# A transformer's band mask moved from TensorE to VectorE, and ten maxima steps ahead instead of eight

## What is computed

```python
k = jnp.repeat(k, 2 * NQ // NKV, axis=1)
scores = jnp.einsum('bhqd,bhkd->bhqk', q, k) / math.sqrt(HD)
scores = jnp.where(causal, scores, -jnp.inf)
aw = jax.nn.softmax(scores, axis=-1)
```

```python
mask = (it < jb) | (it > jb + w) | (jb == -1)          # w = 32
sim = jnp.einsum('bhwie,bhwje->bhwij', bq, bk2) * QK_SCALE
sim = jnp.where(mask, -jnp.finfo(sim.dtype).max, sim)
attn = jax.nn.softmax(sim, -1)
out = jnp.einsum('bhwij,bhwje->bhwie', attn, bv2)
```

## Time and profile before

| | us |
|---|---|
| three executions | 3745.32, 3753.55, 3750.16 |
| median | 3750.16 |
| profiled execution | 3755.21 |
| its span, first to last instruction | 3753.5 |
| second attention in it, about | 1107 to 1622 |
| transformer in it, about | 1695 to 3735 |

### The profile page before, as it was taken

One profiled execution on the slowest core, in us unless ns is written; L12 is line 12 of the kernel. 1 busy time (PEld: TensorE's weight loads), 2 busy tenths in 40 slices (PEclk: granted clock), 3 DMA queues, 4 the chain that ended last, 5 costly groups with the idle time before them and its releaser, 6 DMA issues. The chain is left out here.

```text
span 3753.5 us, 73312 instructions
## 1 busy us (share of the span) xinstructions
PE 3066.9 (82%) x23925; PEld 1648.9 (44%) x23925; DVE 2241.2 (60%) x3755; ACT 2086.3 (56%) x3805; POOL 1286.9 (34%) x1223
## 2 busy tenths in 40 slices
PE   2788886249638888836999999999999999999997
PEld 1332332113312232314665565566556556655653
DVE  6888887652347777764555555545555555555553
ACT  1477676012105666624666666666666666666664
POOL 0000000014225556514543453344335334534540
PEclk6588779579858999978999999999999999999998
DMA  5221121124231211123111111111111111111111
GB/s 198 82 84 53 60 72 67 48 52 112 55 43 28 38 35 34 34 64 104 42 45 42 41 52 30 47 39 48 30 48 53 30 42 44 49 31 52 38 35 41
DMA packets 195374, 200.80 MB, mean 53 GB/s; under 512 B 119109, under 2 KB 125909, under 8 KB 190250
## 3 DMA queue, kind: packets, MB, share of 16 engines
q1 hardware_dynamic: 193938, 195.86, 19.1%
q10 hardware_dynamic: 1080, 0.25, 0.0%
HBM read 100.23 MB, written 29.46 MB: 35 GB/s over the span
## 5 line engine op out<-in xcount | busy, mean ns | idle before, releaser
L2427 POOL TENSOR_TENSOR tr_t<-tr_t 128x512 f32<-128x512 f32 x384 | 488.8, 1273 | 707.4 <-DVE tr_t L2271 707.0
L2434 POOL TENSOR_TENSOR tr_nq<-tr_t,tr_rn 128x512 f32<-128x512 f32 x384 | 392.5, 1044 | 393.4 <-ACT tr_rn L2167 393.4
L1638 DVE TENSOR_REDUCE attn_mp<-attn_ps 128x1 f32<-128x512 f32 (+3 forms) x660 | 394.1, 656 | 143.1 <-PE attn_ps L1494 64.1
L2132 ACT ACTIVATE tr_pr<-tr_ps 128x768 f32<-128x768 f32 x264 | 213.9, 810 | 375.6 <-PE tr_ps L1954 375.2
L2270 DVE TENSOR_TENSOR tr_t<-tr_ps,tr_tab 128x512 f32<-128x512 f32 x384 | 263.3, 686 | 245.8 <-ACT tr_sq L2141 245.8
L2280 DVE TENSOR_TENSOR tr_o<-tr_ps,tr_rd 128x384 f32<-128x384 f32 (+1 forms) x264 | 144.0, 545 | 426.8 <-ACT tr_rd L2157 419.0
L1969 PE MATMUL tr_ps<-tr_w,tr_xs 128*128 128x512 f32 x768 | 372.6, 607 | 29.5 <-DVE tr_xs L2298 26.4
L684 DVE TENSOR_REDUCE attn_mcol<-attn_ps 128x1 f32<-128x512 f32 x548 | 357.4, 682 | 49.4 <-PE attn_ps L529 39.4
L1600 ACT ACTIVATE attn_pr<-attn_ps 128x768 f32<-128x768 f32 (+2 forms) x352 | 295.3, 870 | 150.7 <-PE attn_ps L1521 149.8
L668 ACT ACTIVATE attn_pr<-attn_ps 128x512 f32<-128x512 f32 x512 | 272.7, 600 | 88.1 <-DVE attn_ps L706 68.9
L1954 PE MATMUL tr_ps<-tr_qT,tr_kT 64*128 64x96 f32 (+1 forms) x4224 | 301.8, 283 | 0.0
(11 more groups left out here) (260 smaller groups left out, 5082.7 us busy)
## 6 DMA issues: line engine op xcount, KB each, us to landing
tr_v<-tr_va SPq DMA_DIRECT2D x144, 192.0 KB, 2.6
attn_ka<-scratch_kp SPq DMA_DIRECT2D x72, 294.0 KB
tr_v<-tr_va SPq DMA_DIRECT2D x144, 128.0 KB, 2.4
moe_cb<-scratch_combineT SPq DMA_DIRECT2D x32, 512.0 KB
tr_w<-in_w_half SPq DMA_DIRECT2D x12, 1024.0 KB
tr_v<-tr_va SPq DMA_DIRECT2D x48, 256.0 KB, 2.4
scratch_kp<-proj_parts SPq DMA_DIRECT2D x36, 256.0 KB
attn_km<-scratch_kp SPq DMA_DIRECT2D x72, 98.0 KB
```

What stands on the lines that cost most here:

```text
L1638: dve.tensor_reduce(dst, src, AX.X, ALU.max).then_inc(maxed, 1)
L2427: pool.tensor_tensor(t12[:, slot, i, 0, :], t12[:, slot, i, 0, :], t12[:, slot, i, 1, :], ALU.add).then_inc(summed, 1)
L2434: pool.tensor_tensor(nq[:, slot, i, :].rearrange("p (h e) -> p h e", e=DH), t12[:, slot, i, 0, :].rearrange("p (h e) -> p h e", e=DH), rn[ ...
```

## The change

In the transformer the mask matmuls go. `scores` starts its own accumulation and waits for `masked` of the step before instead of `exp_done`. VectorE gets a new `mask(n, j, s)`, first in its step: it adds `band` (now f32, one copy, broadcast over the two banks) to the scores in PSUM and writes 128 x 768 into `pr`. ScalarE's `exps` now waits for `masked`, works in place in `pr`, and stands after `copy_v` instead of at the head of the step. The second load of the band, its cast and `stage_ident` go.

In the second attention `LEAD_STEPS` is 10 instead of 8, and `negate_rows` stands at a = 14, behind the output's copy, instead of at a = 16.

```diff
-LEAD_STEPS = 8
+LEAD_STEPS = 10
...
                         elif a == 14:
                             copy_out(2 * kv + 1, 1, kv)
-                        elif a == 16:
+                        if a == 14:
                             negate_rows(kv + 1, (s + 1) % 2, kv)
...
-        band32 = st.sb("band32", [P, 2, 2, NPAIR * QT])
-        band = st.sb("band", [P, 2, 2, NPAIR * QT], BF16)
+        band = st.sb("band", [P, 2, NPAIR * QT])
...
-            sp.dma_start(band32[:, 0, :, :], d["band"]).then_inc(loaded_const, 16)
-            for half in range(2):
-                sp.dma_start(band32[half * DH:(half + 1) * DH, 1, :, :], d["band"][(1 - half) * DH:(2 - half) * DH]
-                             ).then_inc(loaded_const, 16)
+            sp.dma_start(band[:], d["band"]).then_inc(loaded_const, 16)
...
-                at_least(pe, exp_done, NQT * n + s)
+                at_least(pe, masked, NQT * n + s)
...
-                pe.sem_inc(scores_begun, 1)
-                for e in range(2):
-                    for half in range(2):
-                        row, out = half * DH, (half ^ e) * DH
-                        pe.matmul(ps[out:out + DH, SC0 + e, 0:NPAIR * QT], identb[row:row + DH, row:row + DH],
-                                  band[row:row + DH, e, 1 if s == 0 else 0, :], start=True, stop=True,
-                                  tile_position=(row, out), skip_group_check=True)
...
-                                       qT[rows, p, s * QT:s * QT + width], start=False, stop=True,
-                                       skip_group_check=True)
+                                       qT[rows, p, s * QT:s * QT + width], start=True, stop=True)
...
             def exps(n, j, s):
-                act.wait_ge(scores_done, NQT * n + s + 1)
-                act.activation(pr[:, (j + s) % 2, :, :], ps[:, SC0:SC0 + 2, 0:NPAIR * QT], ACT.Exp,
-                               scale=QK_SCALE).then_inc(exp_done, 1)
+                act.wait_ge(masked, NQT * n + s + 1)
+                act.activation(pr[:, (j + s) % 2, :, :], pr[:, (j + s) % 2, :, :], ACT.Exp, scale=QK_SCALE
+                               ).then_inc(exp_done, 1)
...
                 for s in range(NQT):
-                    exps(n, j, s)
...
                         copy_v(n + 1, PROJ_NEXT_AT[s])
+                    exps(n, j, s)
...
+            def mask(n, j, s):
+                dve.wait_ge(scores_done, NQT * n + s + 1)
+                seen = band[:, 1 if s == 0 else 0, :].unsqueeze(1).broadcast_to((P, 2, NPAIR * QT))
+                dve.tensor_tensor(pr[:, (j + s) % 2, :, :], ps[:, SC0:SC0 + 2, 0:NPAIR * QT], seen, ALU.add
+                                  ).then_inc(masked, 1)
...
                 for s in range(NQT):
+                    mask(n, j, s)
                     if s:
                         outputs(n, s - 1)
...
-            dve.wait_ge(loaded_const, 96)
-            link(dve.tensor_copy(band[:], band32[:]))
+            dve.wait_ge(loaded_const, 64)
```

More of the change, by code:

```diff
@@ L1797, in tile_width, with stage_transformer @@
     return min(QT, S - t * QT)
-def stage_transformer(nc, d, ident, identb, yT):
+def stage_transformer(nc, d, ident, yT):
     with Stage(nc, "tr") as st:
@@ L1845, in stage_transformer @@
         summed, nq_ready, turned, qk_ready = S_("summed"), S_("nq_ready"), S_("turned"), S_("qk_ready")
-        scores_done, exp_done, scores_begun = S_("scores_done"), S_("exp_done"), S_("scores_begun")
+        scores_done, exp_done, masked = S_("scores_done"), S_("exp_done"), S_("masked")
         v_done, v_copied = S_("v_done"), S_("v_copied")
@@ L2483, in build @@
             stage_stash(nc, d, xT, sT)
-        inner, si = scope()
-        with inner:
-            identb = si("identb2", [P, P], BF16)
-            stage_ident(nc, ident, identb)
-            stage_transformer(nc, d, ident, identb, xnT)
-        stage_final(nc, d, ident, xnT)
-def stage_ident(nc, ident, identb):
-    with Stage(nc, "ident") as st:
-        block = st.block()
-        @block.vector
-        def _(dve):
-            dve.tensor_copy(identb[:], ident[:])
+        stage_transformer(nc, d, ident, xnT)
+        stage_final(nc, d, ident, xnT)
 def stage_stash(nc, d, xT, sT):
```

## The result

The change makes the kernel faster: a median of 3706.85 us in four executions (3705.62 to 3709.09) against 3750.66 in four of before, a ratio of 0.9885 with a 95% interval of 0.9868 to 0.9903. The forecast was 3709. A second measurement of the same kernel, later on, gave 3713.69 against 3751.73 (0.9899, 0.9884 to 0.9914). The profiled execution took 3709.1 us, its span is 3707.4.

The account below looks back on a forecast made before the run. TensorE's order was taken to bound the transformer stage, more than half the span. Terms -76.6 + 39.2 - 4 - 3.4 + 4 = -40.8, off the median 3750.16, gave 3709 us; 8-in-10 range 3684 to 3738.

Parts of the forecast that it names:

- gain of the mask: Transformer, TensorE: without the four mask matmuls each of 264 steps saves 0.29 us, -76.6 us.
- new wait: Transformer: TensorE waits for the exponential, now behind the values' copy, in 67 steps at 0.59 us on average, +39.2 us.
- give-back: Transformer, step 3 of 11 feeding passes: the exponential no longer delays ScalarE's key copy, 0.4 us each, -4 us.
- second attention: Second attention: sooner rows gain 0; two more maxima steps and a wait for the negation cost +4 us together.
- start of the stage: Transformer's start: the small cast stage, one band transfer and the band's cast go, -3.4 us.
- VectorE's addition: Transformer: VectorE's mask addition takes 0.96 us a step and TensorE does not wait for it, 0 us.
- 0.1 us on top for weights not loaded ahead: Transformer, steps with TensorE's wait for the exponential: weights load late after it, 0.1 us beyond the 0.51 us wait.
- price of 1.38: VectorE's mask addition: alternative time of 1.38 us, from a multiplication with both inputs in SBUF, instead of 0.96.
- Rival D: Transformer: the in-place exponential from SBUF is much dearer and the 67 waits grow; 3766 at 1.55 us; chance 0.05.
- Rival C: Second attention: the maxima rows do arrive sooner and the 26.9 us wait goes, 3682; chance 0.05.
- Covered steps shorter by 0.29: Sign in the transformer's profile: steps of kind 3 shrink by 0.29 us; less than 0.2 would refute the prediction.
- Attention within 10 us: Sign in the second attention: if it moves by more than 10 us, the prediction is wrong.

Follow-up runs that it names:

- no_mask: The kernel before without the four mask matmuls of a step, exponential scaled by 1e-6 and left at the step's head: 3678.42 us, ratio 0.9807.
- exp_mid: The whole change, but the exponential of steps 2 (not feeding), 6, 8 (h = 0) and 10 stands between squares and values' copy: 3679.93 us, ratio 0.9813.
- mask_twice: The whole change with VectorE's addition made twice in every step, once into a buffer nobody reads: 3710.21 us, ratio 0.9900.
- tr_rows_first: The change's transformer with the second attention of before, SyncE issuing the maxima row transfers ahead of the second output's store: 3672.33 us, ratio 0.9799.

## Why the prediction was right, and where it was lucky

The total was met to 2 us (the later measurement to 5), inside the range, and that is in part luck. The mechanism of the transformer half held, but the gain of the mask was 6 us too high, the new wait 8 too dear and the give-back 5 too small, while the second attention cost 4 to 12 us more than its term and the end of the stage 2.4 that had none; these errors cancel. Here is what each term came to in the traces.

| term | predicted | measured |
|---|---|---|
| mask matmuls | -76.6 | -70.5 (no_mask, step lengths) |
| give-back from the exponential's move | -4 | -8.7 (exp_mid against no_mask) |
| new wait | +39.2 | +31.5 (after against exp_mid) |
| start of the stage | -3.4 | -5.0 |
| VectorE's addition | 0 | 0 (mask_twice) |
| second attention | +4 | +7.8 in the traces, 10 to 16 in the runs |
| after the last scores | not in the sum | +2.4 |

Each of the first three is the difference of two single profiles, and they add up to the stage's -47.7 by their making.

**Mask.** The 0.29 us a step is right. It was counted in all 264, and in steps 0 and 3 of the feeding passes TensorE waits for another engine, which takes most of it back. The give-back in those steps 3 was 0.65 us, not 0.4. The two terms together are -79.2 against -80.6, so the mistake was one of attribution: of what was left in step 3 the exponential's place decides.

**The new wait.** Place, cause and the kinds of steps (2, 6, 8, 10) were right: steps 3, 7, 9 and 0, in which it shows, grow by 0.14 to 0.23 against the kernel before, while nearly all others shrink by 0.29. The copy of the values starts 0.18 us after the scores where 0.19 was worked out, the exponential takes 0.849 where 0.845 was, and the wait is 0.50 where 0.51 was. What failed is the 0.1 us on top for weights not loaded ahead, taken from the earlier trace rows: the lengths show 0.50 and 0.43 (step 6), not 0.61 and 0.54. Nor is the count quite that of the sum: behind step 10 the next step 0 is 0.37 us longer than in `exp_mid` in 22 of 23 passes, the rounds' ends among them, where the sum had 0.59 in 18. The output projections of the earlier trace rows differ by 0.11; the denominators pay nothing of the kind, and why the two differ was not tested. By kinds the change against `exp_mid` is 6.3 us in step 3, 10.1 in step 7, 5.9 in step 9 and 8.5 in step 0, 30.7 of the measured 31.5. That the sum's own 43 x 0.50 + 24 x 0.43 = 31.8 comes so close is partly chance.

**VectorE.** The addition takes 0.950 us, 0.96 was worked out, while GpSimd is busy beside it for 868 of the stage's 1920 us. This agrees with what the Trainium skill, SBUF — State Buffer, Who interferes with whom, says of a VectorE instruction with one SBUF input. The price of 1.38 from the row with two was far off. That the addition is hidden holds even at double the price.

**ScalarE's source.** In place from SBUF the exponential takes 849 ns; from PSUM, in the groups of before, it took

```profile
L2132 ACT ACTIVATE tr_pr<-tr_ps 128x768 f32<-128x768 f32 x228 | 184.7, 810 | 326.8 <-PE tr_ps L1954 326.4
```

so 39 ns more. 35 came from the rows. The 52 cycles of the Trainium skill, VectorE: DVE Perf Modes, The TRN2 errata, make an estimate of 43; the trace lies between. Rival D is out.

**The start.** The constants are there 8.9 us after the first issue (1698.14 to 1707.08) instead of 10.65, close to the 1.6 worked out, and both casts are gone. The rest is 0.5 us of a semaphore behind the cast, 0.6 of a shorter gap between the stages, and 0.4 on the way to the first scores. That gap is not chance: from the end of the combination to the first issue, without the cast stage's 0.84, it is 7.9 us in all seven kernels with ten steps ahead and 8.2 to 8.5 in the six with eight. Why is open.

Before, then after:

```profile
1707.55 1.87 DVE L2398 MEMSET tr_xs<- 128x2176 f32 x1 [0.52 <-DVE tr_band L2397]
```

```profile
1698.14 0.34 SPq L1876 DMA_DIRECT2D tr_rope<-in_rope  x1
1707.08 1.87 DVE L2392 MEMSET tr_xs<- 128x2176 f32 x1 [20.14 <-DMA tr_band<-in_band]
```

**The second attention** is the step that failed, +4 where the runs say 10 to 16. Its two pieces were sized well: the prologue grew by 3.0 us (2.7), and the wait of a maxima step for the negation is 9.3 us in 16 places, 0.58 each (0.7). Nor is the sentence that this comes out of the wait for the rows what failed in the main. Before, beside the 26.9 us of the earlier trace rows, the first scores waited

```profile
PE attn_ps L1521 <- issue: 3.3, 1, 3.3
```

so 30.2 us in all, and in the change 22.3 (11.1 and 11.2): 7.9 of the 9.3 us came out of it, though only ten heads and not 14 still wait for the rows by name.

What failed is that the sum stops there: it puts the effect of the two steps on a head's first units at nothing, without a reason. The reasoning was that SyncE's queue ends last, which is true, so that time lost on TensorE in a head is hidden. But that queue is not free-running: it starts at the copy of the first output, which hangs on TensorE's first units. In a head without slow units its store starts 6.00 us after the head's first scores in the kernel before and 6.21 in the change; from there SyncE needs 20.4 to 23.1 us to the last row transfer before and 20.4 to 22.7 after, and in most heads the next scores come 1.1 after that in both. The stage is a ring through TensorE, ScalarE and SyncE: what comes behind the first output's copy, as the wait for the negation does, can be hidden, and what is put into the first units is paid. Summed over the 16 heads, the time from the first scores to the end of that copy is 108.5 to 115.0 us in the six profiles with ten steps ahead and 102.0 to 106.8 in the three with eight. The means are 6.7 apart; with 3.7 for the prologue that is 10.4 of the 14.8 us, and where the other 4.4 arise was not settled.

About half of the 6.7 is the 0.21 in each head, 3.4 us. The other half goes with the clock. Two heads' first units in the change, and the stores of their first outputs:

```profile
1174.50:1182.50 8.00, 7.71 (x56) 2.49 (x58) 4.75 (x8) 3.77 (x4) 3.44 (x4) 0.57 0.00 1
1206.40:1211.80 5.40, 5.05 (x57) 2.12 (x57) 4.38 (x8) 3.66 (x4) 3.35 (x3) 1.00 0.00 0
```

```profile
1183.31 1.71 SPq L1356 DMA_DIRECT2D scratch_o<-attn_ob  x4
...
1212.59 1.69 SPq L1356 DMA_DIRECT2D scratch_o<-attn_ob  x4
```

Ahead of the first TensorE had been idle for 2.28 us, ahead of the second for 1.24. The granted clock is 0.57 in the one, so mostly at 1.2 GHz, and 1.00, 2.4 GHz, in the other, and the first output's store starts 8.75 us after the first scores instead of 6.21. That is so in four of the change's six slow heads; in the other two it is 7.3. In the kernel before a slow head was usually 0.9 to 1.4 us later there, at most 2.2, but twelve heads were slow. So in this pair all that slow heads lose there against the others is no more in the change (12.5 us) than in the kernel before (13.5); over all the profiles it is 12.4 to 19.0 with ten steps and 9.3 to 14.2 with eight. The order of ten steps puts more of TensorE's work in front of the first output; that this is why its slow heads are slower fits the traces, but was not tested by itself. Rival C was the right mechanism attached to the wrong edit: the rows could arrive sooner, by their place in SyncE's list and not by a sooner negation.

**After the last scores.** The last step's exponential now waits for the addition and stands in the open: TensorE waits 1.99 us for it where it waited 1.24 for VectorE's outputs. The rest goes with the clock: 0.90 in the last 35 us of the stage before, 0.80 after.

```profile
3651.33 0.87 PE L1976 MATMUL tr_ps<-tr_pr,tr_ones 128*64 128x384 f32 x4 [1.99 <-ACT tr_pr L2120]
```

```profile
3655.00:3690.00 35.00, 24.64 (x48) 8.88 (x46) 9.73 (x16) 10.16 (x13) 0.00 (x0) 0.80 0.00 0
```

**The lines that were to show it.** No mask matmuls: yes. Covered steps shorter by 0.29: yes. Some 67 idles of 0.5 us: 58 in 21 of the 24 passes, 70 in all. Rows wait in some 14 heads: 10, and 3 more at the rounds' ends are now put down to "issue". Attention within 10 us: yes in the one pair of profiles; in the runs the second half costs 10 to 16, and the nine profiles' means are 14.8 apart. By the prediction's own words that part was wrong.

## What to carry to other kernels

Work that is moved off the bounding engine brings its new dependencies along: ask at which place of the helping engine's list its result is ready just in time, and what is pushed back by it. The same exponential cost 31.5 us at the end of the step, about twice that ahead of the squares, and nothing that the step lengths show between the squares and a copy that waits anyway. When a queue "ends last", look up what starts it: if it is released by the engine you think is covered, there is no cover. And a list of DMA issues is worth reading for items that stand ahead of the urgent one without need; that swap was the cheapest gain here, 15 to 29 us.

## What was not expected of the hardware

- A transfer's issue is dear next to what it moves: four row transfers of 2.0 KB each occupy SyncE for 2.8 us and four stores for 1.7 to 2.2. In the second attention, at 34 GB/s, the order of these issues sets the pace: the row transfers ahead of one store are worth 15 to 29 us.
- The end of a loop round leaves TensorE idle for 2.6 to 4.7 us in front of its next matmul, in all these kernels, also where the last row transfer was issued over 4 us before (2.6 to 2.8 in `tr_rows_first`). The profile mostly puts it down to "issue":

```profile
1386.88 0.57 PE L1521 MATMUL attn_ps<-attn_qt,attn_kh 64*128 64x512 bf16 x2 [3.83 <-issue]
```

  The Trainium skill, Runtime: NRT & Kernel Launch, Instruction fetch mechanics, says that a taken branch out of the fetched pages stalls until its target has been fetched; the row fits that, but no run here takes the loop away.
- The same stage of the same code varied between 536.6 and 544.0 us from one kernel to the next. Eight of the 16 heads began at a lower clock in the first, ten and twelve in the two at 544.0; by the first output's copy this had cost 9.3 us against 14.2 and 13.5, some two thirds of the difference.
